# First attention of a two-layer network on one core: aggregate and gate kept feature-major, norms and factor by products with TensorE

## The reference, cut to what matters

```python
qg = split_heads(tokens @ Wqg, HEADS);  kv = split_heads(tokens @ Wkv, HEADS)
queries, gates  = qg[..., :DIM_KEYS], qg[..., DIM_KEYS:]
keys, values    = kv[..., :DIM_KEYS], kv[..., DIM_KEYS:]
queries, keys, values = l2norm(queries), l2norm(keys), l2norm(values)
attn = square(relu(einsum('bhid,bhjd->bhij', queries, keys)))
aggr = einsum('bhij,bhjd->bhid', attn, values)
out  = tanh_norm(aggr) * tanh(silu(gates))      # tanh_norm(t) = tanh(|t|) * t / max(|t|, 1e-12)
return merge_heads(out) @ Wout
```

## Time and profile before

| | us |
|---|---|
| median of three runs | 1882.21 (1878.13 to 1887.14) |
| the profiled execution, its own time | 1882.32 |
| its span, from the first to the last instruction | 1880.5 |
| the attention stage's residual additions, first to last of 16 | 490.0 to 1199.7 |

### The profile page before, as it was taken

One profiled execution on the slowest core, in us unless ns is written; L12 is line 12 of the kernel. 1 busy time (PEld: TensorE's weight loads), 2 busy tenths in 40 slices (PEclk: granted clock), 3 DMA queues, 4 the chain that ended last, 5 costly groups with the idle time before them and its releaser, 6 DMA issues.

```text
span 1880.5 us, 28307 instructions
## 1 busy us (share of the span) xinstructions
PE 1255.7 (67%) x8634; PEld 880.8 (47%) x8635; DVE 1244.0 (66%) x2728; ACT 727.4 (39%) x1190; POOL 1018.8 (54%) x1176
## 2 busy tenths in 40 slices
PE   3435333478777777877787779257767776746796
PEld 1223122236666565656665558223433333325685
DVE  6788850177787878787878873167777778743322
ACT  1101001145454454454444553036565555532221
POOL 2356576456666666666666645334445444425554
PEclk7555555578888888888888887669898889878766
DMA  4010004400000000000000000210000000001110
GB/s 132 22 27 15 13 13 81 94 7 1 8 8 8 7 6 6 6 6 6 6 3 3 7 4 6 72 33 12 19 18 16 9 17 17 7 17 44 42 40 12
DMA packets 73354, 40.91 MB, mean 22 GB/s; under 512 B 23811, under 2 KB 68716, under 8 KB 73284
## 3 DMA queue, kind: packets, MB, share of 16 engines
q1 hardware_dynamic: 50530, 24.02, 4.6%
q0 software_dynamic: 20384, 11.67, 3.1%
q10 hardware_dynamic: 2370, 4.35, 0.8%
HBM read 31.11 MB, written 23.87 MB: 29 GB/s over the span
## 4 chain that ended last, share of the span: by engine, by line
PE 33%; DVE 29%; issue 13%; POOL 13%; ACT 7%; DMA 2%; ACTq 1%; POOLq 1%; SPq 0%; DVEq 0%; another core or an unknown queue 0%
PE psum L1138 9%; PE psum L1189 5%; POOL xe_dram L570 4%; DVE terms L1766 4%; DVE o L1606 4%; PE psum L1246 3%; POOL o_inv L618 3%; DVE q_highT L1792 2%; PE psum L1166 2%; POOL got L768 2%; POOL out L777 2%; PE psum L1304 1%; DVE rden L1458 1%; PE psum L1269 1%; DVE silu_g L1700 1%
## 5 line engine op out<-in xcount | busy, mean ns | idle before, releaser
L1138 PE MATMUL psum<-v,attn 128*128 128x64 f32 x2048 | 287.8, 300 | 25.6 <-ACT aggr L870 17.1
L1138 PEld LDWEIGHTS psum<-v,attn 128*128 128x128 f32 x2048 | 271.9, 213 | 61.1 <-issue 44.2
L1766 DVE TENSOR_REDUCE terms<-psum 128x4 bf16<-128x1024 f32 x128 | 156.9, 1226 | 45.5 <-PE psum L1269 43.7
L641 POOL DMA_INDIRECT yg<-ye_dram,routel x128 | 140.1, 1095 | 60.0 <-issue 36.2
L945 ACT ACTIVATE prob<-psum 128x512 f32<-128x512 f32 x256 | 139.5, 602 | 49.7 <-PE psum L1233 45.5
L570 POOL DMA_INDIRECT xe_dram<-rows_out,route x128 | 131.8, 1030 | 39.6 <-issue 39.0
L855 ACT ACTIVATE attn<-psum 128x1024 f32<-128x1024 f32 x128 | 129.9, 1015 | 10.1 <-PE psum L1121 8.9
L1147 PE MATMUL psum<-ident,o 128*128 128x128 f32 x256 | 48.7, 353 | 117.9 <-DVE silu_g L1700 91.0
L618 POOL TENSOR_TENSOR o_inv<-o_max,minus_half 128x16 f32<-128x16 f32 x32 | 107.6, 3364 | 2.7
L658 POOL TENSOR_TENSOR v<-v,inv 128x2048 f32<-128x2048 f32 x16 | 70.7, 4418 | 59.8 <-DVE inv L1586 59.8
L1147 PEld LDWEIGHTS psum<-ident,o 128*128 128x128 f32 x256 | 39.1, 183 | 131.5 <-DVE o L1606 66.5
(11 more groups left out here) (300 smaller groups left out, 3106.5 us busy)
## 6 DMA issues: line engine op xcount, KB each, us to landing
x4n_dram<-x4n SPq DMA_DIRECT2D x16, 256.0 KB, 4.5
w<-in_w POOLq DMA_DIRECT2D x48, 64.0 KB, 2.3
x_in<-in_x SPq DMA_DIRECT2D x8, 256.0 KB, 2.9
xe_dram<-zero_rows SPq DMA_DIRECT2D x8, 256.0 KB, 3.2
x_dram<-x1s SPq DMA_DIRECT2D x8, 256.0 KB, 2.4
xe_dram<-rows_out,route POOLq DMA_INDIRECT x128, 2.1
xe<-xe_dram SPq DMA_DIRECT2D x16, 128.0 KB, 2.4
ye_dram<-ye SPq DMA_DIRECT2D x16, 128.0 KB, 2.2
```

Source lines behind the costliest of these rows:

```text
L641: pool.indirect_dma_start(yg[fetch.p][:, j, k, :], None, ye_dram, bass.IndirectOffsetOnAxis(ap=where[:, j, K0 + k:K0 + k + 1], axis=0), bo ...
L1138: mm = pe.matmul(psum[:, 4 + j, (head % HALF) * DV:(head % HALF + 1) * DV], attn[g % RING][:, h, c * SEQ + j * P:c * SEQ + (j + 1) * P], v ...
L1766: dve.tensor_reduce(dst[:, :, 2 * m2:2 * m2 + 2], psum[:, 4:6, :].rearrange("q p (b k) -> q p b k", b=2), AX, ALU.max, negate=True).then_i ...
```

## The change

Values, aggregate and gates change their orientation; the work per sequence stays the same.

- `aggregate`: the head's 64 value columns are now stationary and 256 columns of the squared scores move. The result is feature-major: the two heads of a pair lie in partitions 0 to 63 and 64 to 127 of one bank half, and two pairs fill a bank. Four blocks b = 0 to 3 a sequence, in bank 4 and 5 by turns.
- ACT squares a bank straight out of PSUM (`square_aggregate`); the copy `aggr` is gone. The sum over a head's 64 features is a product on PE (`norms_of`): a 128x128 piece of the squares stationary, the 128x2 block of ones `pair_ones` moving. DVE copies the 16 columns to `o_norm` (`take_norms`).
- DVE multiplies gate and aggregate out of PSUM (`gate_aggregate`) before the norms are known. POOL only makes the factor (`factor`). PE spreads it over the features (`spread_factor`): one column of `o_factor`, repeated 64 times, is stationary, the identity moves. DVE multiplies that out of PSUM into `oT` (`scale_output`).
- The transposes of `o` with their two copies, DVE's sum L1601, and POOL's scaling of the gate L630 are gone.
- The gate product has the weights stationary and the tokens moving. The output product too, so its result is feature-major; ACT copies it (`y3T`), PE transposes it back, and DVE adds the residual in g = 7 instead of 6.
- The value copies go from DVE to ACT (`take_v`).
- The order by g is new: DVE makes the first two silu pieces in g = 4, behind `inverse_root`, the other two in g = 5; POOL issues three of the eight gathers after its second square; ACT's tanh of the norms of hf 1 stands in g = 4 behind the square of att's block 0.
- One more weight is loaded (`pair_ones`, 17 instead of 16 transfers).

The diff, cut to its core:

```diff
@@ POOL
-            def scale_gate(q, hf):
-                hold(s["gate_made"], 2 * q.n)
+            def factor(q, hf):
+                hold(s["factor_ps"], 4 * (q.n - 1) + 2 * hf)
                 hold(s["o_tanh_made"], 2 * (q.n - 1) + hf + 1)
                 pool.tensor_tensor(o_factor[:], o_tanh[:], o_inv[:], ALU.mult).then_inc(s["o_factor_made"], 1)
-                for j in range(2):
-                    ins = pool.tensor_tensor(part, part, o_factor[...].to_broadcast([P, HALF, DV]), ALU.mult)
...
             def half(fetch, front, att, tail):
+                if tail:
+                    factor(tail, 0)
                 if fetch:
...
+                    gather(fetch, PLACES[0:5])
+                if att:
+                    square(att, POOL_PAIRS[0])
                 if tail:
                     length_of(tail, 1)
                 if att:
-                    square(att, POOL_PAIRS[0])
+                    square(att, POOL_PAIRS[1])
+                if fetch:
+                    gather(fetch, PLACES[5:])
                 if tail:
-                    scale_gate(tail, 1)
-                if att:
-                    square(att, POOL_PAIRS[1])
+                    factor(tail, 1)
                 if front:
...
-                if att:
-                    length_of(att, 0)
...
                 if att:
-                    scale_gate(att, 0)
-                if att:
                     square(att, POOL_PAIRS[2])
+                    length_of(att, 0)
@@ ACT
+            def square_aggregate(q, b):
+                wait(act, s["norm_ps"], 2 * (q.n - 1) + b // 2)
+                act.wait_ge(s["attn_read"], PAIRS * (q.n - 1) + 2 * b + 2)
+                act.activation(aggr_sq[:, b % 2, :], bank[4 + b % 2], ACT.Square).then_inc(s["aggr_sq_made"], 1)
+            def take_v(front, g):
+                for h in range(2):
...
+                    act.activation(v[front.p][:, g - 1, 512 * h:512 * h + 512], ring[1 - h][:], ACT.Copy).then_inc(s["v_copied"], 1)
+                    act.wait_ge(s["v_copied"], m)
+                    square_of(front, 2 + 2 * (g - 1) + h, v[front.p][:, g - 1, 512 * h:512 * h + 512])
...
+                    if att and g == 4:
+                        square_aggregate(att, 0)
+                    if tail and g == 4:
+                        tanh_of_norm(tail, 1)
@@ PE, aggregate
-                for j in range(2):
+                for c in range(2):
                     for h in range(2):
                         head = 2 * g + h
-                        for c in range(2):
-                            mm = pe.matmul(psum[:, 4 + j, (head % HALF) * DV:(head % HALF + 1) * DV], attn[g % RING][:, h, c * SEQ + j * P:c * SEQ + (j + 1) * P],
-                                           v[q.p][:, c, head * DV:(head + 1) * DV], start=(c == 0), stop=(c == 1))
+                        mm = pe.matmul(psum[DV * h:DV * h + DV, 4 + b % 2, (g % 2) * SEQ:(g % 2 + 1) * SEQ], v[q.p][:, c, head * DV:(head + 1) * DV],
+                                       attn[g % RING][:, h, c * SEQ:(c + 1) * SEQ], start=(c == 0), stop=(c == 1))
@@ PE, new
+            def norms_of(q, hf):
+                b = fill(1, [(s["o_norm_made"], ...)], [(s["aggr_sq_made"], 4 * (q.n - 1) + 2 * hf + 2)])
+                for j in range(2):
+                    for a4 in range(4):
+                        at = (a4 % 2) * SEQ + j * P
+                        mm = pe.matmul(b[:, HALF * j + 2 * a4:HALF * j + 2 * a4 + 2], aggr_sq[:, a4 // 2, at:at + P], pair_ones[:], start=True, stop=True)
+            def spread_factor(q, hf):
+                for b2 in range(2):
+                    b = fill(b2, [(s["o_made"], ...)], [(s["o_factor_made"], 2 * (q.n - 1) + hf + 1)] if b2 == 0 else [])
+                    for a2 in range(2):
+                        for j in range(2):
+                            for h in range(2):
+                                at = HALF * j + 4 * b2 + 2 * a2 + h
+                                mm = pe.matmul(b[DV * h:DV * h + DV, a2 * SEQ + j * P:a2 * SEQ + (j + 1) * P], o_factor[:, at:at + 1].to_broadcast([P, DV]), ident[:], start=True, stop=True)
@@ PE, half
+                    if tail and g == 1:
+                        spread_factor(tail, 0)
+                    if tail and g == 3:
+                        norms_of(tail, 1)
                     if front and g in (3, 4):
                         for h in range(2):
-                            b = fill(G_BANK[g - 3][h], [(s["silu_made"], m)], [])
-                            pe.matmul(b[:], x3T[:, (g - 3) * P:(g - 2) * P], w_g[:, 512 * h:512 * h + 512], start=True, stop=True).then_inc(s["g_ps"], 1)
+                            b = fill(h, [(s["silu_made"], m)], [])
+                            for a2 in range(2):
+                                mm = pe.matmul(b[:, a2 * SEQ:(a2 + 1) * SEQ], w_g[:, pair * P:(pair + 1) * P], x3T[:], start=True, stop=True)
...
                     if tail and g == 5:
-                        turn_oT(tail, 1)
+                        spread_factor(tail, 1)
...
+                    if tail and g == 6:
+                        for c in range(PAIRS):
+                            mm = pe.matmul(b[:, 0:SEQ], w_out[:, c, :], oT[:, c // 2, (c % 2) * SEQ:(c % 2 + 1) * SEQ], start=(c == 0), stop=(c == PAIRS - 1))
+                    if att and g == 6:
+                        norms_of(att, 0)
+                    if tail and g == 7:
+                        for j in range(2):
+                            mm = pe.transpose(b[:, j * P:(j + 1) * P], y3T[:, j * P:(j + 1) * P], ident[:])
@@ DVE, half (g by g)
+                    if tail and g == 0:
+                        gate_aggregate(tail, 2)
+                    if tail and g == 2:
+                        scale_output(tail, 0)
+                        scale_output(tail, 1)
+                    if tail and g == 3:
+                        gate_aggregate(tail, 3)
+                        take_norms(tail, 1)
                     if front and g == 3:
                         v_sum(front, 2)
                         v_sum(front, 3)
                         inverse_root(inv3[:], norm3[:], 6 * HEADS, s["inv_made"])
...
+                    if front and g in (4, 5):
+                        for h in range(2):
...
+                            dve.scalar_tensor_tensor(silu_g[g - 4][:, 512 * h:512 * h + 512], tanh_g[h][:], 1.0, ring[h][:], ALU.add, ALU.mult).then_inc(s["silu_made"], 1)
+                    if att and g == 4:
+                        gate_aggregate(att, 0)
                     if front and g == 5:
                         split_terms(front)
                     if tail and g == 5:
-                        take_oT(tail, 1)
+                        scale_output(tail, 2)
+                        scale_output(tail, 3)
+                    if att and g == 6:
+                        gate_aggregate(att, 1)
+                    if att and g == 6:
+                        take_norms(att, 0)
```

More of the change, by code:

```diff
@@ L323, in build_program @@
         silu_g = two("silu_g", [P, HEADS * DV])
-        gate = two("gate", [P, 2, HEADS * DV])
+        gate = two("gate", [P, 4, 2 * SEQ])
         RING = 4
         attn = [sb(f"attn{n}", [P, 2, 512]) for n in range(RING)]
-        aggr = sb("aggr", [P, 2, 512])
-        aggr_sq = sb("aggr_sq", [P, 2, 512])
-        o = sb("o", [P, 2, 512])
-        oT = sb("oT", [P, 2, PAIRS, P])
+        aggr_sq = sb("aggr_sq", [P, 2, 2 * SEQ])
+        o = sb("o", [P, 4, 2 * SEQ])
+        oT = sb("oT", [P, 4, 2 * SEQ])
+        y3T = sb("y3T", [P, SEQ])
         x3 = two("x3", [P, 2, D])
@@ L666, in half @@
                 if att:
-                    scale_gate(att, 0)
-                if att:
                     square(att, POOL_PAIRS[2])
-                chain.restart()
+                    length_of(att, 0)
+                if fetch or att or tail:
+                    chain.restart()
             pipeline(pool, half)
@@ L891, in half @@
                     if tail and g == 0:
-                        take_aggregate(tail, 1)
+                        tanh_of_norm(tail, 0)
                     if tail and g == 2:
-                        tanh_of_norm(tail, 1)
+                        square_aggregate(tail, 3)
                     if front and g in (1, 2):
-                        for h in range(2):
-                            act.wait_ge(s["v_copied"], 4 * (front.n - 1) + 2 * (g - 1) + h + 1)
-                            square_of(front, 2 + 2 * (g - 1) + h, v[front.p][:, g - 1, 512 * h:512 * h + 512])
+                        take_v(front, g)
                     if front and g in (3, 4):
@@ L925, in half @@
                                        ring[0].bitcast(F16).rearrange("q (a j t) -> q a j t", a=4, j=2), ACT.Copy).then_inc(s["qkT_act"], 1)
+                    if tail and g == 6:
+                        act.wait_ge(s["y3T_ps"], tail.n)
+                        act.activation(y3T[:], ring[0][:, 0:SEQ], ACT.Copy).then_inc(s["y3T_made"], 1)
```

(37 more changed lines are left out.)

145 lines of the change are left out of this document (61 added, 84 removed).

## The result

The changed kernel takes 1907.0 us (median of four runs, 1901.4 to 1913.2) against 1882.0 (1878.1 to 1887.1): 1.0132 times as long, 95% interval 1.0087 to 1.0177. Slower by 1.3%, as forecast (1914), inside the range. The profiled execution took 1913.2 us with a span of 1911.6; that of before had a span of 1880.5, so the traces differ by 31.1 us.

The account below looks back on a forecast made before the run. Waits between in-order streams, no engine a wall, were taken to bound the kernel. A half of 52.0 us against 49.7, 14 x 2.3 = +32 us, filling and draining cancelling, gave 1914 us, range 1857 to 1985.

Parts of the forecast that it names:

- S0: First score product of a half on PE, taken as t = 0; the next one forecast at 51.1 or 52.0 us.
- S3: Fourth score product of the half on PE, forecast 1.2 us earlier than its 14.3 us before.
- stall inside the inverse root: DVE's inverse root held up while POOL squares pair 3, claimed at 1.9 us a half.
- The middle: Stretch from the silus to the terms: second gates 4.2 us at the lower clock, spread from 33.4, terms from 39.0.
- the split: DVE's `split_terms`: first product stands until 36.1 behind POOL's value scaling, a 2.2 us stall; whole step ends at 38.2.
- The tail: End of the half on PE, terms at 39.0 to next score product at 51.1; 0.9 us more if the lower clock lasts.
- the walk: The forecast's step-by-step order of PE through one half, giving 52.0 us against 49.7.
- The tie: POOL's value scaling against DVE's square of pair 4, within 0.1 us; the other way all is 1.3 us later.
- Filling and draining: First and last halves: filling ones lose some 3 us each, the two draining gain about as much; net nothing.
- slower still: Rival: PE's clock stays low through terms and output product; a half near 57 us, 1987 us in all; chance 0.20.
- About even: Rival: clock full from the second gates on (1872 us), or norm products at half cost (1888 us); chance 0.18.
- Faster: Rival: POOL's pair 3 square and value scaling miss DVE's work; a half of 47.9 us, 1857 us; chance 0.20.

Follow-up runs that it names:

- x32: Norm products of a half-sequence made twice with the same values, against the changed kernel: 1985.0 us, 1.0575 of before.
- seven gathers ahead: Changed kernel with two silus ahead of the inverse root, pair 3's square ahead of the length, seven gathers (not five) before pair 2's square: 1803.4 us.

## Why the prediction was right

Counted from S0 of the half shown (761.64), forecast against trace: S3 at 13.1 and 12.85; norm products 1.9 us and 1.95; `take_norms` done at 16.7 and, 777.88 + 0.17, at 16.4, after a DVE wait of 4 and 3.98 us; stall inside the inverse root 1.9 and 1.57; pause before the second gates 5.4 and 5.23; the gates 4.2 and 3.78 (the forecast's x16 for them is x8 in the trace, 1.97 us at the higher level, near its 2.1 us); second spread from 33.4 and 31.95; terms from 39.0 and 37.7; output product ended at 45.0 and 43.2; next S0 at 51.1, or 52.0 with the 0.9 us added for the clock, and 52.3. Fourteen times 2.3 us was the sum; thirteen halves gave 2.4.

Three terms were off, and they offset each other; that the sum is within 7 us of the measured time is in part luck. *The middle* came 1.3 to 1.8 us early, since the stall was 1.57 us and not 1.9, the gates at the lower level took 3.78 and not 4.2, and the split ended that much sooner. *The tail* lost it again: I put it all at full clock, but from 805.61 on the clock is down (0.59 from 805.50 to 818.00) and the aggregate takes 1.97 us, the terms 1.89; and the second norm products wait 0.80 us for the copy of kT, which the walk did not have. *The tie* of value scaling and DVE's square falls either way, as the text said, and on its bad side DVE's square stands 3.4 us, where 1.3 was written. The two kinds of halves still come out within 2 us of each other: on the bad side the split is free, PE has no wait for the copy of kT, and its tail runs at the higher level (aggregate 1.08 us, terms 1.07). That the walk's kinder side stands for both is luck too.

*Filling and draining* I put at +3 each and as much back. The first residual addition is 14.0 us later, the last two halves are shorter by 15.0: right in the sum, too small in each. Of the 14.0 about 5 us are the addition's own move from g = 6 to 7 (in before it stands 5.3 us ahead of the next S0, at 495.28, in the half of after shown 0.3 us); the rest was not followed up.

Of the rivals, *slower still* was right that the tail sees the lower level again, and wrong in where and how long: no half of after is above 53.2 us, since PE's level is back when the output product begins (3.72 us in after, 5.89 before) and falls only behind it, in some of the halves. *About even* needed a full clock behind the pause, and the rows show 3.78; the kernel that keeps PE at work gets it for the gates and comes out at the 1872 of this rival, though with halves of 49.5 us and not 49.0. *Faster*, with POOL's two steps missing DVE, named the right place. Its 1857 us for both steps is reached by moving one of them, the value scaling, alone (1856).

The norm products were the term with no row. The Trainium skill, "TensorEngine Tiling (Array Packing)", section Instruction Overhead, puts a product with few moving columns at some 60 cycles, from which the forecast estimated 0.4 us. The trace does not agree: 1.84 to 1.95 us for x16 and 3.63 for x32 at the higher level, so the nearest row, the old aggregate with its fresh weights, was the better guide.

## What to carry to other kernels

When an edit turns one engine's step into another engine's wait, list what stands behind that wait in its stream: here a 0.17 us copy of norms, waiting 3.98 us for PE, held back an inverse root and, behind it, the silus on which TensorE's next work hung, and some 148 us less of busy time on two engines bought nothing until the order was changed. Price a meeting of VectorE and GpSimd by both sides of the tie, and look for a stretch in which one of them waits anyway. And gains of separate reorderings do not add: after each one read again what PE waits for, since the step moved out of one wait (the value scaling ahead of the factor) can be the next one's cause.

## What the runs showed of the hardware

POOL's power on 16 elements per partition, 2.93 us long, does not hold up DVE: in the stretch 778.59 to 781.53 of after DVE's small steps, some with two SBUF operands, take 0.21 to 0.26 us. POOL's products on 1024 or 2048 elements do: 1.83 us for such a step. The Trainium skill, "SBUF — State Buffer", section "SBUF: two separate sides", says that of a DVE instruction with two SBUF inputs and a GpSimd instruction whichever starts first holds the ports that they share for its whole instruction. The rows agree for the wide products, both ways (3.4 us of stall for DVE, 1.1 for POOL, by 0.07 us of order), and not for the power, whose span in the profile is longer than what it blocks.

TensorE's granted clock fell from its higher level (2.4 GHz) to its lower (1.2) in a stretch in which PE was busy without a gap, nearly all of it with norm products of two moving columns (5.50 us busy of 5.50, mean clock 0.70); the same x32 in another place ran at the higher level throughout (3.63 us). It is not bound to these products: with seven gathers ahead the first gates, 256 moving columns, took 3.61 us from 685.63 instead of 1.97, with PE busy for all of 683.80 to 690.50 (6.70 of 6.70 us, mean clock 0.75). What tells such places apart was not tried.
